# Second attention of a gated block: softmax sums per head, and where the normalised delta is formed

## What is computed

```python
x = x + tanh(g_xattn[0]) * L0_xattn(layernorm(x), ctx_2048, mask_bk0)
x = x + tanh(g_ffn[0])   * L0_ffn(layernorm(x), w1, w2, w3)          # quantised activations, sign weights
x = x + tanh(g_xattn[1]) * L1_xattn(layernorm(x), ctx_2048, mask_ik0, Wq, bq, Wk, bk, Wv, bv, Wo, bo, ...)
x = x + tanh(g_ffn[1])   * L1_ffn(layernorm(x), w_gate, w_up, w_down)

# inside L1_xattn: 16 heads of 16 columns
scores = clip(q @ k.T / sqrt(16), -50, 50)      # masked keys: -50
probs  = softmax(scores)
delta  = min(max(residual_scale, 0), 0.3) * ((probs @ v) @ Wo.T + bo)
L1_xattn = (delta - mean) / sqrt(var + 1e-5) * ln_gamma + ln_beta
```

## Time and profile before

| | before |
|---|---|
| median of 3 runs | 263.72 us (263.62 to 264.2) |
| profiled execution, its time | 264.11 us |
| profiled execution, its span | 262.3 us |
| busy share of the span: PE, DVE, ACT, POOL | 81%, 69%, 51%, 32% |
| mean granted clock of PE, share of full speed | 0.946 |

### The profile page before, as it was taken

How to read it: one execution, slowest core, us unless ns; L and a number is a source line. 1 busy time by engine, 2 the same in 40 slices (tenths; PEclk the granted TensorE clock), 3 DMA queues, 4 the chain that set the end, 5 groups by cost and what they waited for, 6 DMA issues and landing times.

```text
span 262.3 us, 4538 instructions
## 1 busy us (share of the span) xinstructions
PE 212.0 (81%) x1658; PEld 174.5 (67%) x1658; DVE 181.0 (69%) x457; ACT 132.8 (51%) x296; POOL 83.9 (32%) x108
## 2 busy tenths in 40 slices
PE   0285557979889889897798688775999999999992
PEld 0264325858778778786576466654877888888882
DVE  2769879598988988786428999998984333262333
ACT  1138874478667667679755455553322323222220
POOL 2301111175856856868505333442100000000000
PEclk9999955699999999999959999997999999999999
DMA  5999003900000000000000000000000000020002
GB/s 169 369 390 301 5 0 139 343 1 0 2 0 0 2 1 0 2 2 0 0 2 2 0 2 4 0 4 0 2 2 0 0 0 2 0 80 2 0 0 80
DMA packets 9238, 12.55 MB, mean 48 GB/s; under 512 B 1025, under 2 KB 7937, under 8 KB 9217
## 3 DMA queue, kind: packets, MB, share of 16 engines
q1 hardware_dynamic: 8784, 12.07, 13.3%
q10 hardware_dynamic: 432, 0.20, 0.4%
HBM read 11.22 MB, written 1.05 MB: 47 GB/s over the span
## 4 chain that ended last, share of the span: by engine, by line
PE 50%; DVE 27%; ACT 7%; DMA 6%; issue 4%; POOL 3%; SPq 1%; DVEq 0%; ACTq 0%; POOLq 0%
PE PB L1259 16%; PE PB L1278 7%; DMA WRAW<-w_dram 6%; PE PB L1073 6%; PE PB L1172 4%; PE PB L1085 3%; DVE XV L524 3%; PE PB L1108 2%; PE PB L1112 2%; DVE HBQ L742 2%; PE PB L1019 2%; DVE RD L728 2%; DVE HBQ L572 2%; ACT SIL L906 2%; DVE HSD L578 2%
## 5 line engine op out<-in xcount | busy, mean ns | idle before, releaser
L1259 PE MATMUL PB<-SGN,WHI 128*128 128x512 f32 x128 | 40.5, 397 | 0.0
L1073 PE MATMUL PB<-SGN,XQH 128*128 128x512 f32 x64 | 27.7, 433 | 1.3 <-DVE XQL L553 1.3
L699 DVE TENSOR_TENSOR WRAW<-WRAW,PB 128x512 f32<-128x512 f32 x16 | 11.0, 686 | 24.0 <-ACT WRAW L993 23.9
L1278 PE MATMUL PB<-WHI,SGN 128*128 128x256 f32 x128 | 25.6, 283 | 2.2 <-DVE SGN L707 1.8
L1073 PE MATMUL PB<-SGN,XQL 128*128 128x512 f32 x64 | 27.1, 424 | 0.0
L289 POOL TENSOR_TENSOR RSTD<-MVS,MHALF 128x1 f32<-128x1 f32 x24 | 13.4, 560 | 40.9 <-DVE MVS L401 40.9
L1259 PEld LDWEIGHTS PB<-SGN,WHI 128*128 128x128 f32 x128 | 22.9, 188 | 4.5 <-issue 0.2
L1259 PE MATMUL PB<-SGN,WLO 128*128 128x512 f32 x64 | 25.2, 394 | 0.0
L993 ACT ACTIVATE WRAW<-PB 128x512 f32<-128x512 f32 x16 | 9.6, 600 | 28.0 <-PE PB L1259 28.0
L1278 PEld LDWEIGHTS PB<-WHI,SGN 128*128 128x128 f32 x128 | 20.7, 188 | 3.6 <-DVE SGN L707 2.4
L316 POOL TENSOR_TENSOR HBQ<-HBQ,HR 128x512 f32<-128x512 f32 x16 | 17.6, 1098 | 17.2 <-DVE HR L590 17.2
(11 more groups left out here) (122 smaller groups left out, 545.7 us busy)
## 6 DMA issues: line engine op xcount, KB each, us to landing
WRAW<-w_dram SPq DMA_DIRECT2D x2, 2048.0 KB, 12.1
X<-x_dram SPq DMA_DIRECT2D x2, 512.0 KB, 5.8
CTXT<-ctxt_dram SPq DMA_DIRECT2D x1, 1024.0 KB, 9.6
CTX<-ctx_dram SPq DMA_DIRECT2D x1, 1024.0 KB, 12.0
WRAW<-w_dram SPq DMA_DIRECT2D x1, 1024.0 KB, 14.9
WQK<-wqkvo_dram SPq DMA_DIRECT2D x1, 1024.0 KB, 7.8
WRAW<-wd_dram SPq DMA_DIRECT2D x1, 1024.0 KB, 10.1
out_dram<-X SPq DMA_DIRECT2D x4, 256.0 KB, 2.2
```

The source lines that it names most:

```text
L1073: mm = nc.tensor.matmul(PB[2 * half + m][:], part[:, p, c, :], sgn(m, c, a, b), start=(c == 0 and k == 0), stop=(c == DC - 1 and k == 1))
L1259: mm = nc.tensor.matmul(PB[2 * b + m][:], wcol(w_part, m, c, j), act_part[:, c, g * TG:(g + 1) * TG], start=(c == 0 and i == 0), stop=(c = ...
L1278: mm = nc.tensor.matmul(down_bank(g, k), act_part[:, b, ts], wdown(w_part, j), start=(j == 0 and i == 0 and k % 2 == 0), stop=(j == FC - 1 ...
```

## The change

- Sums: each head's sum is made once. 32 matmuls of 64 columns with zero-one weights `SEL` gather the sums of 16 heads and two halves of the rows into 128 partitions by 64 columns of bank 7 (`head_sums`). DVE takes the reciprocal of 64 columns in place of 256. Four matmuls with zero-one weights `SPREAD` (128 x 128, from the identity) then spread the reciprocals over the value columns, into the other half of bank 7 (`spread_sums`). ACT copies the weighted values to SBUF (`values_out`), and DVE multiplies the two.
- Normalised delta: DVE makes the negated mean `NM2`, POOL the product `OFF2` = NM2 * RSTD2, ACT forms D1 = DL * RSTD2 + OFF2 (`centred`), and POOL multiplies by gamma and adds to X.
- Order: X is updated one step later, so `norm_d`, its transposition (now in bank 6), `hi_d` and `lo_d` stand three tiles behind in place of two, and the last two of them move between the groups of the fourth stage. ACT takes all four exponentials of tile 0 ahead of the pipeline, and those of tile t + 1 in step t. The banks of `down_d` are swapped accordingly.

```diff
-            ones2 = ONE2[:].rearrange("p e d -> p (e d)")
-            nc.gpsimd.memset(ones2[:, 0:HD], 1.0).then_inc(set_pool, 1)
...
+            nc.gpsimd.memset(SEL[:], 0.0).then_inc(set_pool, 1)
+            pool.wait_ge(set_pool, 4)
+            for r in range(2 * CT4):
+                nc.gpsimd.memset(SEL[:, r, r:r + 1], 1.0).then_inc(set_pool, 1)
+            nc.gpsimd.memset(SEL[:, 0, 2 * CT4:], 1.0).then_inc(set_pool, 1)
...
+            pool.wait_ge(ld["ident"], 16)
+            for c in range(DC):
+                for half in range(2):
+                    at = 4 * c + half
+                    rows = ident[:].rearrange("p (j s) -> p j s", s=HB32)[:, :, at:at + 3:2]
+                    nc.gpsimd.tensor_copy(
+                        SPREAD[:, 2 * c + half, :].rearrange("p (j e d) -> p j e d", e=2, d=HD),
+                        rows.unsqueeze(3).broadcast_to([P, CT4, 2, HD])).then_inc(set_spread, 1)
```

POOL's step:

```diff
             def step_c(t, p):
                 if live(t - 2):
-                    rstd(t - 2, t - 2 + 2 * NT)
+                    pool.wait_ge(c_ve, t - 1)
+                    nc.gpsimd.tensor_tensor(RSTD2[:], VE2[:], MHALF[:], ALU.pow
+                                            ).then_inc(c_r2, 1)
+                    pool.wait_ge(c_r2, t - 1)
+                    nc.gpsimd.tensor_tensor(OFF2[:], NM2[:], RSTD2[:], ALU.mult
+                                            ).then_inc(c_of, 1)
+                if live(t - 3):
+                    rstd(t - 3, t - 3 + 2 * NT)
                 if live(t + 1):
                     v_tile(t + 1, 1 - p)
+                if live(t - 2):
+                    pool.wait_ge(c_d1, t - 1)
+                    nc.gpsimd.tensor_tensor(D2[:], D1[:], GAM[:], ALU.mult).then_inc(c_d2, 1)
+                    pool.wait_ge(c_d2, t - 1)
+                    pool.wait_ge(c_xb, t - 1)
+                    nc.gpsimd.tensor_tensor(X[:, t - 2, :], X[:, t - 2, :], D2[:], ALU.add
+                                            ).then_inc(x_done, 1)
...
-                if live(t - 1):
-                    pool.wait_ge(c_ve, t)
-                    nc.gpsimd.tensor_tensor(RSTD2[:], VE2[:], MHALF[:], ALU.pow
-                                            ).then_inc(c_r2, 1)
```

DVE's step, and its loop of the fourth stage:

```diff
             def step_c(t, p):
+                if t == NT:
+                    gu_d(0)
                 if live(t - 1):
                     dve.wait_ge(c_dn, t)
-                    nc.vector.reciprocal(RD[:], PB[7][:, 0:D]).then_inc(c_rd, 1)
+                    nc.vector.reciprocal(RD[:], PB[7][:, 0:P // 2]).then_inc(c_rd, 1)
                 if live(t + 2):
                     norm(t + 2, p, 2)
-                if live(t - 1):
-                    dve.wait_ge(c_rd, t)
-                    dve.wait_ge(c_pv, t)
-                    need(dve, c_dl, t - 1)
-                    nc.vector.tensor_tensor(OT[:], PB[6][:, 0:D], RD[:], ALU.mult
+                if live(t - 3):
+                    norm_d(t - 3)
+                if t == NT:
+                    lo_gu(0)
+                if live(t - 1):
+                    dve.wait_ge(c_sp, t)
+                    dve.wait_ge(c_pc, t)
+                    nc.vector.tensor_tensor(OT[:], PV[:], PB[7][:, D:2 * D], ALU.mult
                                             ).then_inc(c_o, 1)
-                if live(t - 2):
-                    norm_d(t - 2)
                 if live(t):
 
                     dve.wait_ge(c_ex, 4 * t + 4)
...
+                if live(t - 3):
+                    lo_d(t - 3)
                 if t == NT:
-                    gu_d(0)
-                    lo_gu(0)
+                    stats(t - 2, p, t - 2 + 2 * NT)
+                    gu_d(1)
                 if live(t - 1):
                     dve.wait_ge(c_dl, t)
+                    need(dve, c_d1, t - 1)
...
+                    need(dve, c_of, t - 1)
+                    nc.vector.tensor_scalar(NM2[:], MV2[:, 0:1], -1.0, None, ALU.mult
+                                            ).then_inc(c_nm, 1)
                     nc.vector.tensor_scalar(VE2[:], MV2[:, 1:2], LN_EPS, None, ALU.add
                                             ).then_inc(c_ve, 1)
-                if live(t - 2):
-                    lo_d(t - 2)
-                if live(t - 1):
-                    nc.vector.scalar_tensor_tensor(
-                        out=D2[:], in0=DL[:], scalar=MV2[:, 0:1], in1=GAM[:],
-                        op0=ALU.subtract, op1=ALU.mult).then_inc(c_d2, 1)
...
-                    nc.vector.scalar_tensor_tensor(
-                        out=X[:, t - 1, :], in0=D2[:], scalar=RSTD2[:], in1=X[:, t - 1, :],
-                        op0=ALU.mult, op1=ALU.add).then_inc(x_done, 1)
-                    stats(t - 1, 1 - p, t - 1 + 2 * NT)
...
+                if t == NT:
+                    lo_gu(1)
+                elif live(t - 2):
+                    stats(t - 2, p, t - 2 + 2 * NT)
...
             for n in range(2, NG * FC):
                 gu_d(n)
+                if n in (2, 4):
+                    norm_d(NT - 3 + n // 2)
+                if n in (3, 5):
+                    lo_d(NT - 3 + n // 2)
                 lo_gu(n)
                 if n == 2:
-                    lo_d(NT - 1)
+                    stats(NT - 1, 1, 3 * NT - 1)
```

ACT's step and its fourth stage:

```diff
+            def values_out(u):
+                act.wait_ge(c_pv, u + 1)
+                need(act, c_o, u)
+                nc.scalar.copy(PV[:], PB[6][:, 0:D]).then_inc(c_pc, 1)
+
+            def centred(u):
+                act.wait_ge(c_of, u + 1)
+                need(act, c_d2, u)
+                nc.scalar.activation(D1[:], DL[:], ACT.Identity, bias=OFF2[:], scale=RSTD2[:]
+                                     ).then_inc(c_d1, 1)
+
             def step_c(t, p):
-                if live(t):
-                    exp_c(t, p, 0)
-                    exp_c(t, p, 1)
                 if live(t + 1):
                     q_out(t + 1)
-                if live(t):
-                    exp_c(t, p, 2)
-                    exp_c(t, p, 3)
+                if live(t - 2):
+                    centred(t - 2)
+                if live(t - 1):
+                    values_out(t - 1)
+                if live(t + 1):
+                    exp_c(t + 1, 1 - p, 0)
+                    exp_c(t + 1, 1 - p, 1)
                 if live(t + 2):
                     copy_ht(t + 2, p, 4, xt_done, c_q, c_ht, 2 * NT)
-                if live(t - 2):
-                    hi_d(t - 2)
+                if live(t - 3):
+                    hi_d(t - 3)
+                if live(t + 1):
+                    exp_c(t + 1, 1 - p, 2)
+                    exp_c(t + 1, 1 - p, 3)
...
+            for b in range(4):
+                exp_c(0, 0, b)
             pipeline(step_c, lag=0)
...
+            for n in range(NG * FC):
+                if n in (3, 5):
+                    hi_d(NT - 3 + n // 2)
                 silu_d(n)
+                if n == 0:
+                    centred(NT - 2)
                 hi_gu(n)
+                if n == 0:
+                    values_out(NT - 1)
+                    hi_d(NT - 3)
+                if n == 1:
+                    centred(NT - 1)
```

PE's new functions and its step:

```diff
+            def head_sums(u, p):
+
+                pe.wait_ge(c_p, u + 1)
+                for c in range(DC):
+                    for e in range(2):
+                        for half in range(2):
+                            r = (2 * c + e) * 2 + half
+                            for j in range(CT4):
+                                at = head_at(HPC * c + 2 * j + e) + half * (P // 2)
+                                mm = nc.tensor.matmul(
+                                    PB[7][HB32 * j:HB32 * (j + 1), 0:P // 2], SEL[:, r, :],
+                                    PR[:, p, at:at + P // 2], start=(r == 0),
+                                    stop=(r == 2 * CT4 - 1))
+                mm.then_inc(c_dn, 1)
...
+            def spread_sums(u):
+
+                pe.wait_ge(c_rd, u + 1)
+                for k in range(2 * DC):
+                    at = D + k * (P // 2)
+                    mm = nc.tensor.matmul(PB[7][:, at:at + P // 2], SPREAD[:, k, :], RD[:],
+                                          start=True, stop=True)
+                mm.then_inc(c_sp, 1)
...
+            def xd_t(u):
+                pe.wait_ge(d_ln, u + 1)
+                pe.wait_ge(c_pc, min(u + 3, NT))
+                need(pe, d_hl, u)
...
+                if t == NT:
+
+                    pe.wait_ge(c_ex, 4 * NT)
+                    gate_up_d(0)
+                if live(t - 1):
+                    head_sums(t - 1, 1 - p)
+                    head_values(t - 1, 1 - p)
+                if live(t - 1):
+                    spread_sums(t - 1)
                 if live(t + 1):
                     scores(t + 1, 1 - p)
                 if live(t + 2):
                     xt_c(t + 2, p)
+                if live(t - 3):
+                    xd_t(t - 3)
                 if t == NT:
                     gate_up_d(1)
                 if live(t - 1):
```

(77 more changed lines are left out.)

47 lines of the change are left out of this document (19 added, 28 removed).

## The result

The changed kernel takes 260.88 us (median of four runs, 259.28 to 261.53), the kernel before 263.96 beside it: 3.1 us less; ratio 0.9862, 95% interval 0.983 to 0.9894 (the two medians alone give 0.9883). The profiled execution took 261.3, with a span of 259.5 against 262.3.

A forecast was written before the change was run, and what follows sets the result against it. PE bounds half the span, DVE 27%, with DVE gapless in the 7.20 us steps. Terms -0.3 - 2.5 - 0.3 + 1.0 = -2.1 gave 262.0, as a median 261.6 us; range 258.0 to 265.3.

The forecast's parts named there:

- Start: Stretch before the steps: second reciprocal at 144.1 against 144.37, with the clock falling to half again; -0.3 us.
- clock kept: Rival: the clock doesn't fall at the start, or is back earlier; second reciprocal at 140.9, 258.4 us in all; chance 0.20.
- Five steps: Second to seventh reciprocal: a step falls from 7.20 to 6.92 us, 36.91 to 34.4 in all; -2.5 us.
- waits of 0.66 and 1.15: In each step DVE waits 0.66 us before OT and some 1.15 before `lo_d`.
- The price of the spread: On PE, eight 128x128 weight loads at 0.107 us each at full clock, 0.86 us per spread; bounds 0.43 and 1.28.
- To the end of the first gates: Seventh reciprocal to the end of the first gate and up group: 6.43 us becomes 6.1; -0.3 us.
- tail: End of the first gate and up group to the end of the sixth: 24.43 us becomes 25.4; +1.0 us.
- Both forecast waits for `norm_d`: In the tail, PE waits twice for `norm_d`, which now stands behind `gu_d`; 0.6 us each.
- sums by their starts: Rival: the 64 sums matmuls cost 27 ns per start, 1.74 us each time; PE's step 7.5, 265.3 us in all; chance 0.17.
- POOL holds DVE off: Rival: in the steps, the clamp beside POOL's two passes is held, losing 1.44 us; +0.3 in six steps, 263.4; chance 0.13.
- The cover I gave: In a step, POOL's two passes end about 3.5 us after the reciprocal starts; DVE reads X again at 6.2.

The follow-up runs named there:

- Experiment 5: The changed kernel with 16 extra matmuls into an unread bank in PE's two gaps ahead of the first steps: 259.4 us, ratio 0.9799.
- experiment 2: The changed kernel with the statistics of X moved on DVE from the end of a step to ahead of `lo_d`: 260.63 us, ratio 0.989.
- experiment 3: The changed kernel with the sums part undone (256-column sums and reciprocal, no spread), the delta part kept: 264.79 us, ratio 1.0042.
- experiment 8: The changed kernel with old sums and no spread, POOL's gamma product ahead of the values' tile, its additions to X after the clamp: 259.44 us, ratio 0.9807.
- Experiment 1: The changed kernel with the spread matmuls issued twice, the second time over the same result: 268.3 us, ratio 1.0143.
- experiment 6: The changed kernel with the last tiles' two normalisations ahead of the gate product on DVE instead of behind it: 258.76 us, ratio 0.9796.
- experiment 7: The changed kernel with the first gate and up group issued on PE one step earlier, ahead of tile 6's spread: 259.85 us, ratio 0.9825.

## Why the prediction was right

The forecast was 261.6, the median is 260.88, and the chain that it forecast for a step is the one in the trace. Term by term:

- *Start, -0.3 expected, R2 at 144.1: measured 143.66, -0.71.* The half clock came, as forecast from the earlier trace rows. Experiment 5 prices it at 2.89 in the start, and experiment 2, with the change's own instructions there and no fall, at 2.90; the rival "clock kept" put R2 at 140.9 and run 5 had it at 141.31, with a second stage that ended 0.54 later. That it did fall in the profiled execution was no certainty (it stayed up in experiments 2, 3 and 8): that this term came out is in part luck.
- *Five steps, -2.5 expected: measured -2.86.* The chain through spread, scores, exponentials, `hi_d` and `lo_d` was the right one, 6.92 expected and 6.85 measured, and so were its terms: reciprocal 0.55, spread and change of shape 1.00 (measured 1.03 to the scores' start), sums 0.9 (0.92), waits of 0.66 and 1.15 (0.41 and 1.03). The waits are shorter than forecast because DVE's own part of a step is 5.41 (6.85 less both) and not 5.07; that difference lies beside the chain and costs nothing. Experiment 1 shows that the spread stands on it. Of the -2.86, 0.58 was taken in unseen: it is the half clock of before at 180 us, which sat in the 36.91 that I subtracted from.
- *The price of the spread, 0.107 each.* The right size, but not from the row that it was read from. I took the 0.42 of two matmuls as 0.21 each; in the trace the second of them starts 0.07 after the first, and the rest is its own length, so that row gives no pace. The eight instructions of the spread in after start 0.11 apart. That the two agree is luck, as far as that row goes.
- *To the end of the first gates, -0.3: measured 6.43 to 6.15*, and *tail, +1.0: measured 24.43 to 25.38.* The chain of waits of after, in order of time:

```profile
181.06 2.80 PE PB L1334 x12
...
196.31 0.42 DVE XD L740
...
205.53 0.42 DVE XD L740
...
206.44 2.80 PE PB L1334 x12
```

The sixth group ends at 206.44 + 2.80 = 209.24, 25.38 after the first (183.86). Both forecast waits for `norm_d` are in the chain, and experiment 6 prices them at 1.12 together, against my 2 x 0.6.
- *Rival "sums by their starts".* Fell: 64 matmuls in 0.92 are 14 ns each, half the 27 that it needed. In the trace of after four of them, one on each quarter of the array, start 7 ns apart, and the next on the same quarter starts 56 ns after the last one there. So for starts over the whole array, as the prediction took it, the measurement decides against the floor of about 25 ns between starts that the Trainium skill states ("TensorE: Matmul & The Clock Gate", section "Wait — 56ns, not 53.3ns?"); for one quarter alone no run here tests it.
- *Rival "POOL holds DVE off".* Fell in the change, but the other way round: the clamp took 1.34 for 1.27 and POOL's addition was held, 1.59 for 0.72, off the path. The cover I gave, POOL's passes done 3.5 after the reciprocal starts and X read again at 6.2, measured 4.0 and 6.1. Experiments 2 and 3 show how thin it is: with the statistics early, or with a reciprocal of the old length, the same hold lies in what sets the step (0.86 of the addition in 7.26, 1.4 of DVE's instructions in 7.58).
- *What the prediction did not ask.* It costed both parts as one and found 6.92. It never asked what the delta part would give without the sums, though its own working had the answer: DVE's 5.07 + 1.20 = 6.27 with no new wait. Measured, once POOL's turns are moved: 6.55. The part that looked like the larger relief (1.20 of 2.23) is the one to leave out.

## What to carry to other kernels

Before you shorten an instruction on the engine that is full, look at where its result goes: here a shorter reciprocal that needs a round through PE gave back more than it saved, and each half of a change is worth its own sum. A measured wait time is cover only for the order it was measured in; after each move, follow the loop through every engine again. Split a trace at fixed events and compare interval by interval: that separated 1 us here, where medians moved by 1 to 4 us with the clock.

## What the runs showed of the hardware that was not expected

- DVE and POOL exclude each other both ways, and it is the one that starts later that is held: DVE's OT 0.94 for 0.41 (experiment 3), POOL's addition 1.59 for 0.72 (after), the clamp 1.82 for 1.27 and then POOL's addition 1.59 behind it (experiment 2; there the clamp's record begins 0.01 before that of POOL's product, but OT still ran on DVE until 164.70, so which of the two was first those starts don't settle). In after, OT with one operand in PSUM kept its 0.42 (158.99) beside POOL's product (158.86 to 159.59); with both in SBUF it did not. The Trainium skill has this rule in "SBUF — State Buffer", section "SBUF: two separate sides": the pair is an exclusive lock, the first to start keeps it for its whole instruction, and only DVE's two-port modes, or two SBUF inputs beside a GpSimd instruction that reads SBUF, ask for it. These rows agree with it, the one of experiment 2 as far as it can tell.
- The fall of the granted clock behind one and the same stretch of instructions differs from execution to execution: the start took 16.39 in after, 15.06 and 15.07 in experiments 6 and 7, and 13.49 in experiment 2, where the clock didn't fall. What decides it is not settled here; with PE kept busy it stayed up in each of the five profiled executions.
